# Extra TensorE products, whose results nobody reads, in front of some waits of a fused conv and attention kernel

## What is computed

```python
x = L0(x)   # layer norm, shifted 7x7 window attention (3 heads), MLP with exact gelu, both residual
x = L1(x)   # layer norm, 24 -> 48, conv 3x3 -> 24, x + silu(y)
t = tokens(x)                                   # (32, 3136, 24)
for l in (2, 3):
    h = relu(bn(ln(t) @ w1.T))                  # 24 -> 48, "mixer", first stage
    X = fft(h, axis=1)                          # over the 3136 tokens
    xr = relu(X.real * rd - X.imag * id + rb)
    xi = relu(X.imag * rd + X.real * id + ib)
    t = t + bn(ifft(xr + 1j * xi).real @ w2.T)  # "mixer", last stage
    t = t + ffn(ln(t))                          # 24 -> 96 -> 24, inputs rounded to fp8 (e5m2)
```

## Time and profile before

| | us |
|---|---|
| median of the runs shown | 3934.07 |
| those three runs | 3927.19, 3934.07, 3943.25 |
| the profiled execution | 3923.4 |
| its span, first to last instruction | 3921.7 |

### The profile page before, as it was taken

One profiled execution on the slowest core, in us unless ns is written; L12 is line 12 of the kernel. 1 busy time (PEld: TensorE's weight loads), 2 busy tenths in 40 slices (PEclk: granted clock), 3 DMA queues, 4 the chain that ended last, 5 costly groups with the idle time before them and its releaser, 6 DMA issues.

```text
span 3921.7 us, 132316 instructions
## 1 busy us (share of the span) xinstructions
PE 3386.2 (86%) x59692; PEld 2353.1 (60%) x59692; DVE 1755.1 (45%) x2866; ACT 1813.4 (46%) x3411; POOL 231.7 (6%) x489
## 2 busy tenths in 40 slices
PE   6988889888898798987989879898798887898988
PEld 4555845658557485474754747547476484664855
DVE  5434364343633446334463444634446334462454
ACT  3543355543554434544345444454444534445354
POOL 4500000000000000000000000000000000000000
PEclk8999999999999899998999989999999998999999
DMA  2231001010010100101001010010100100001000
GB/s 79 61 75 29 3 14 30 19 29 3 15 46 3 28 3 15 46 3 28 3 15 45 3 28 3 15 46 3 28 3 16 45 15 15 3 16 29 20 11 14
DMA packets 25326, 88.39 MB, mean 23 GB/s; under 512 B 18227, under 2 KB 19363, under 8 KB 20795
## 3 DMA queue, kind: packets, MB, share of 16 engines
q1 hardware_dynamic: 23491, 74.72, 8.0%
q0 software_dynamic: 1280, 5.21, 0.5%
HBM read 63.86 MB, written 14.84 MB: 20 GB/s over the span
## 4 chain that ended last, share of the span: by engine, by line
PE 76%; ACT 11%; DVE 6%; issue 5%; SPq 1%; DMA 1%; ACTq 0%; DVEq 0%
PE ps L1043 76%; ACT rs L654 4%; ACT lv L649 4%; DVE area_ty L874 2%; DMA area_ty<-area_hz 1%; DVE xs L1013 1%; SPq L475 1%; ACT area_ty L735 1%; ACT area_ty L741 1%; ACT sq L641 1%; DVE area_ty L1009 0%; ACT area_ty L783 0%; DVE area_ty L963 0%; ACT area_ty L745 0%; SPq L429 0%
## 5 line engine op out<-in xcount | busy, mean ns | idle before, releaser
L874 DVE TENSOR_TENSOR area_ty<-ps,rs 128x448 f32<-128x448 f32 (+2 forms) x416 | 285.0, 685 | 496.4 <-ACT rs L654 496.3
L759 ACT ACTIVATE area_ty<-ps 120x448 f32<-120x448 f32 (+1 forms) x448 | 243.9, 544 | 438.9 <-PE ps L1043 438.9
L985 DVE COPY area_ty<-ps 120x448 f32<-120x448 f32 (+1 forms) x432 | 269.9, 625 | 387.8 <-PE ps L1043 387.8
L1043 PE MATMUL ps<-sq,keep_sb 128*128 128x448 f32 (+1 forms) x832 | 390.6, 571 | 41.7 <-ACT sq L641 35.8
L1043 PE MATMUL ps<-area_hz 32*64 32x147 f32 (+2 forms) x7180 | 363.7, 290 | 72.5 <-DVE area_hz L912 33.4
L759 ACT ACTIVATE area_hz<-ps 112x384 f32<-112x384 f32 (+2 forms) x384 | 191.3, 498 | 484.1 <-PE ps L1043 484.1
L1043 PE MATMUL ps<-area_ty,area_hz 113*64 113x49 f32 (+1 forms) x10240 | 392.8, 250 | 19.3 <-DMA area_ty<-area_hz 16.9
L1043 PEld LDWEIGHTS ps<-area_hz 32*64 32x64 f32 (+2 forms) x7180 | 291.6, 156 | 169.9 <-issue 145.6
L1043 PEld LDWEIGHTS ps<-area_ty,area_hz 113*64 113x64 f32 (+1 forms) x10240 | 331.6, 135 | 98.7 <-issue 98.4
L649 ACT ACTIVATE lv<-ps 128x448 f32<-128x448 f32 (+1 forms) x416 | 218.1, 524 | 358.2 <-PE ps L1043 356.8
L1043 PE MATMUL ps<-keep_sb,area_hz 112*56 112x56 f32 (+1 forms) x12288 | 365.5, 222 | 11.6 <-ACT area_hz L759 11.2
(11 more groups left out here) (108 smaller groups left out, 3987.9 us busy)
## 6 DMA issues: line engine op xcount, KB each, us to landing
area_hz<-f_all SPq DMA_DIRECT2D x16, 2541.0 KB
xw<-x_in SPq DMA_DIRECT2D x8, 1568.0 KB, 6.8
y_out<-xs SPq DMA_DIRECT2D x32, 252.0 KB
f_all<-piece POOLq DMA_DIRECT2D x16, 317.6 KB, 3.3
area_ty<-area_hz SPq DMA_DIRECT2D x256, 4.6 KB
area_hz<-raw_in SPq DMA_DIRECT2D x1, 2894.0 KB, 9.3
g_sb<-g_in SPq DMA_DIRECT2D x2, 1396.5 KB
g_sb<-g_in SPq DMA_DIRECT2D x1, 1470.0 KB
```

What stands on the lines that cost most here:

```text
L759: act.activation(dst, src, ACT.Relu if st in (ST_H, ST_F2) else ACT.Copy).then_inc(sc_kept, 1)
L874: ve.tensor_tensor(o, a, b, ALU.mult, **kw).then_inc(normed, 1)
L985: ins = ve.tensor_copy(dst, src)
L1043: return pe.matmul(o, a, b, start=start, stop=stop)
```

## The change

TensorE gets a helper `keep_busy(bank, n)` that issues n products of the centering matrix with 448 columns of the constant table into a bank, with no semaphore counted at the end. It is called

- in conv, between `center_mix(2)` and `variance_mix(0)`: 2 products into bank 3, behind an added wait until the four adds of group 0 are counted (the bank held their input);
- in the mixer of both layers, in front of the wait for `normed`: 2 products into bank 5;
- in the FFN of both layers, in slot 1, in front of the wait for `normed` of the first way up: 2 products into bank 4;
- in the first layer's FFN, in slots 8 and 9: 1 product each into bank 4. In slot 8 it stands in front of the wait for `ffn_added`; in slot 9 nothing follows but the second mixer, so that its product stands directly in front of that mixer's 2.

That is 12 products in a quad, 24 MATMUL rows, at seven places in front of six waits. Nothing is removed and nothing is moved; the other engines' programs are unchanged.

```diff
--- before.py
+++ after.py
@@ -1056,6 +1056,11 @@
                 pe.wait_ge(su_ve, N_WIN)
                 mm(ps[:, 0, 0:9 * RW], R("d1")[0:CI, :], R("conv")[0:CI, :]).then_inc(su_pe, 1)
 
+            def keep_busy(bank, n):
+
+                for _ in range(n):
+                    mm(ps[:, bank, 0:TT], K("center"), keep_sb[:, 0:TT])
+
             def center(q, which, i, src):
 
                 k = LN_AT[which, i]
@@ -1304,6 +1309,8 @@
                 center_mix(0)
                 center_mix(1)
                 center_mix(2)
+                pe.wait_ge(conv_added, q * GROUPS * CHUNKS + CHUNKS)
+                keep_busy(3, 2)
                 variance_mix(0)
                 move(1)
                 for i in range(1, NT):
@@ -1327,6 +1334,7 @@
                     pe.wait_ge(ve_kept, q * VE_FILLS + vector_fills(n))
 
                 f3 = K("f3").rearrange("p (r n) -> p r n", r=2)
+                keep_busy(5, 2)
                 pe.wait_ge(normed, ln_count(q, LN_AT[LN_MIX(l), NT - 1]))
                 pe.wait_ge(extra, q * 2 + l + 1)
                 for j in range(ST_STEPS[ST_H]):
@@ -1444,6 +1452,8 @@
                     if 0 <= s - 1 < NT:
                         i = s - 1
                         k = q * 2 * NT + l * NT + i
+                        if i == 0:
+                            keep_busy(4, 2)
                         pe.wait_ge(normed, ln_count(q, LN_AT[LN_FFN(l), i]))
                         for m in range(HC):
                             if i >= 1:
@@ -1454,6 +1464,8 @@
                     if s < NT:
                         pe.wait_ge(ve_kept, q * VE_FILLS + vector_fills(step_of(l, ST_FFN, s) + 1))
                         center(q, LN_FFN(l), s, xs)
+                    if l == 0 and s > NT:
+                        keep_busy(4, 1)
                     if l == 0 and 0 <= s - 2 < NT:
                         pe.wait_ge(ffn_added, q * 2 * NT + s - 1)
                         center(q, LN_MIX(1), s - 2, xs)
```

## The result

The changed kernel takes 3893.53 us (median of four, 3880.93 to 3895.20) against 3932.75 for the kernel before: a ratio of 0.9898, interval 0.9875 to 0.992, some 40 us. 3897 was forecast. A second set of runs of the same two kernels gave 0.9919 (0.9902 to 0.9935), some 32 us. The profiled execution of the changed kernel took 3894.57, near its median; that of before lay 9 us under its own, so the two spans differ by only 28.9.

A forecast was written before the change was run, and what follows sets the result against it. TensorE, busy for 86% of the span, was taken as the bound. Gains and filler cost, 21 + 8.0 + 3.0 + 3.2 + 3 - 1.6 = 36.6, so 37 us off the median 3934.07, gave 3897 us, range 3875 to 3922.

The forecast's parts named there:

- The clock is paid for behind the wait: TensorE's waits cost idle time, then slow products behind them; the change can win back only the second.
- Term 1: Second layer's mixer, first stage of 224 rows: 16.2 us of low-clock excess over eight quads.
- Term 3: From variance 0 of the mixer norm to the first mixer: 8.0 us to win back over seven quads.
- Term 4: First layer's mixer, clock low in quads 0 and 4 behind the wait before it: 3.0 us.
- Term 2: From the first FFN's last down product to the second mixer: 9.8 us of excess over eight quads.
- The discount of 5: First FFN's end and second mixer: falls remaining in three of eight quads cost 5 of 26.0 us, leaving 21.
- Term 5: First layer's FFN: 3.2 us for falls before the first way up in quads 1 and 3, 3 for four others.
- The cost of the fillers: At all filled waits: delay by the added products, between -1 and 3 us, taken as 1.6.
- What would show it: Signs: grant about 0.970, second mixer 9.5 us in at least five quads, mixer no later, TensorE busy under 73 us more.
- The rival of the moving fall: First FFN's end: the fall moves on, since slots 5 to 7 stay unfilled; 3917 us, chance 0.13.
- The rival of the late fillers: Second layer's mixer: three fillers at the low clock outlast the wait by 2.2 us; 3956 us in all, chance 0.04.

The follow-up runs named there:

- the second profile: The unchanged changed kernel, run and profiled again against the kernel before: ratio 0.9919 (0.9902 to 0.9935).
- the kernel with the moved fillers: Against the changed kernel, first FFN's end has 1 product in slot 7, 2 in slot 8, none in slot 9: ratio 0.9912.

## Why the prediction held, and where it didn't

- *The clock is paid for behind the wait* (terms 1 to 5): right. The narrow fillers, which are there but don't stream, brought nothing; the same places with 448 columns brought 32 to 40 us.
- *Term 1, the second mixer*, 16.2 at most: 16.3. *Term 3, the mixer norm*, 8.0: 7.5. *Term 4, the first mixer*, 3.0: 3.0. These were the same work timed at both clocks, and they came to half a microsecond or better.
- *Term 2, the way to the second mixer*, up to 9.8: 1.6, and 3.2 in the second profile. This is the term that was mis-sized. I had taken falls in three of eight quads; there was one in all eight, and in six of eight in the second profile. The filler of slot 8 came too late for most of them: in seven quads of the first profile the clock fell behind the idle of 1.28 us in slot 7, which has no filler. In quad 2 it fell behind the 1.75 us that the filler of slot 8 left, and only there did fillers at the low clock hold the mixer up, by 1.0 us. The discount of 5 that I took off terms 1 and 2 was nearly the right sum for the wrong reason, and that is luck: 21 forecast, 17.9 found, 16.3 of it in term 1, which came whole, and 1.6 in term 2.
- *Term 5, the first FFN*, 6.2: 7.8, by luck as well. The falls in the wait before the first way up (quads 1 and 3 of the kernel before, 3.2 us) did go. But the pauses without a wait now lie before the FFNs of quads 1, 3, 5 and 7, where they lay before those of 0, 4 and 6; a first FFN whose low stretch begins before it takes 39.3 to 39.8 us (41.2, 40.9 and 41.5 before). In quads 0, 2, 4 and 5 the clock falls in slot 0, behind the idles of 0.82 and 0.80 us, 1.6 us each. And 1.5 us of the gain is a pause that lay in quad 2 of the kernel before.
- *The cost of the fillers*, 1.6 at the high clock: not to be seen. The idle before the second mixer is 0.10 in seven quads, and the second FFN's stage is 35.0 as before. The one first FFN at 1.00 takes 37.0 for 36.5; but in the kernel without the second mixer's fillers three of them, with the same products in slot 1, take 36.5 to 36.6.
- *What would show it*: the grant came to 0.967 for 0.970, the second mixer was 9.46 in eight quads for five, TensorE's busy time rose by less than 73 us. "The mixer starting no later" failed in quad 2 alone, at the low clock.
- *The rival of the moving fall* was half true, as a mechanism: the falls at the FFN's end did move, from behind slot 8's idle to slot 7 in most quads. It was wrong in its size, since the moved fall is over before the mixer. Why the falls came earlier isn't shown.
- *The rival of the late fillers* was seen once, in quad 2, and smaller: 1.0 us for 2.2, since the clock came back while they ran.
- *One reading was too strong.* The row PEclk of the earlier trace rows doesn't dip in every quad: it has an 8 in the first slice and in four others. The falls of the other quads are seen only in windows of a few microseconds.
- *The Trainium skill's rule on idle gaps* doesn't hold here: idles of 0.80 to 2.5 us between short products brought the clock down. The page "TensorE: Matmul & The Clock Gate" of the Trainium skill, section "Why this matters for your kernels", warns of longer ones only.

## To carry to other kernels

Look at the granted clock behind a wait, not only at the wait: the same stage of work timed in repeats with and without a low stretch gave the price of the falls to half a microsecond over eight repeats. A filler need not prevent the fall to pay; a short low stretch that ends before the dense work left the larger part of the gain. Check each idle ahead of the place, too: the fall may come before the filler. Size the filler to less than the wait at the clock that it may get, and put real work into the idle where the order allows it, since only that wins the idle too.

## What the runs showed of the hardware

The clock of TensorE fell behind idles far shorter than I had looked for: 0.82 and 0.80 us at the start of an FFN, 1.28 in slot 7, 1.01 in slot 8 of the kernel with the moved fillers, each with short products around it. The length of an idle alone doesn't decide it: the same 0.82 and 0.80 us stand in quad 5 of the kernel before, whose first FFN is granted 1.00, and the same program run twice had the fall at the FFN's end in eight quads and in six. And the mean grant alone says little: with twice the products the ratio is 1.0016 at a grant of 0.968, with the single ones 0.9898 at 0.967. Only the stages behind a fall, timed, say what it costs.
